# Six normalisations of a two-layer transformer kernel, computed on GpSimd directly behind their power instead of on VectorE a slot later

## The chip, the cores and the metric

One core of a Trainium2 chip. The metric is the device time of one execution in microseconds. In the rows PE is TensorE, PEld its weight load, DVE VectorE, ACT ScalarE, POOL GpSimd and SP SyncE; SPq is the queue from which SP starts transfers.

## The reference

x has 8 sequences of 256 tokens with 256 features. Layer 0 is a masked cross-attention and a ternary linear map on rounded activations, layer 1 a cross-attention with bias, a GELU network and two norms inside, then a mixture of 8 experts. Each of the four starts from a norm without weights:

```python
def _layernorm(x, axis=-1, eps=1e-05):
    m = jnp.mean(x, axis=axis, keepdims=True)
    v = jnp.var(x, axis=axis, keepdims=True)
    return (x - m) / jnp.sqrt(v + eps)
...
    x = x + _L0_xattn_ref(_layernorm(x, axis=-1), ctx_1024, ctx_1024, mask_Bx1xSxS2_ik1, L0_xattn_W, L0_xattn_b)
    x = x + _L0_ffn_ref(_layernorm(x, axis=-1), L0_ffn_weight)
    x = x + _L1_xattn_ref(_layernorm(x, axis=-1), ctx_1024, fside_Bx16xSxS2_0, L1_xattn_Wq, ...)
    x = x + _L1_ffn_ref(_layernorm(x, axis=-1), L1_ffn_Wr, L1_ffn_W1, L1_ffn_b1, L1_ffn_W2, L1_ffn_b2)
```

Inside layer 1's attention block there are two more, `layer_norm(x, g1, be1)` ahead of the GELU network and `layer_norm(x, g2, be2)` behind it. These six are what the change is about.

## The kernel before

**Stages.** The layers come first, for all 8 sequences; then routing (softmax of the logits, a threshold search, the placing of the tokens); then eight experts, one after another, each gathering its tokens by an indirect transfer and adding its result to the output.

**Segments, units, slots.** The attention of one sequence in one layer is a segment: A0 to A7 for layer 0, C0 to C7 for layer 1, in the order A0 A1 A2 C0 A3 C1 A4 C2 A5 C3 A6 C4 A7 C5 C6 C7. A segment has 16 units of two heads and 128 queries. Each engine runs a loop over slots; in slot t PE computes the scores of unit t+2 (ps_s, L383), the transposes of unit t's probabilities (ps_t, L393) and the products with the values of unit t-2 (ps_o, L413); DVE adds mask or bias to the scores of t+2 and finds the row's minimum of the negated scores (neg, neg_max, L659), then the low part of the transposed probabilities of t (p_lo, L666); ACT takes the exponentials of t+1 (probs, L810) and the high part of t (p_hi, L817). Every fourth slot ACT copies eight heads' results (o_raw, L896) and POOL normalises them in three operations (L1023, L1026, L1034) into attn.

**Work beside the units.** Everything else is placed in slots by hand, in `slots_of(b)`: the queries and keys of the next segments, output maps, the quantised map, the GELU network. Each engine's program is written in the order of the slots, an engine takes its instructions strictly in this order, and semaphores order the engines against each other.

**The norms.** Each has a letter: A ahead of layer 0's queries, B ahead of the Hadamard map, C ahead of layer 1's queries, F ahead of the GELU network, G behind it, R ahead of the router. A norm has four steps for a pair of tiles of 128 tokens. DVE: BATCH_NORM_STATS and BATCH_NORM_AGGREGATE (L618, L622), which give mv, mean and variance. POOL: `po_rstd` (L918), an addition of eps and a power of -0.5 (L921, L923) on 128x2 elements. DVE, one slot later (R of b up to 4: three): `ve_ln_apply` (L628), two TENSOR_SCALAR of 128x256 (L633) that subtract the mean and multiply by rstd. Then the user. PE transposes nrm A, B, C, F and R (L327). For G, POOL multiplies by g2 and adds be2 (L1007, L1010) and adds the result to x (L1014), which raises x3_ready.

**Who stands behind x3_ready.** DVE takes R's statistics from this x. SP, whose program is also in slot order, stores x (L1561), and its next transfers follow in its queue: for a later segment, part_h and part_l (the high and low half of keys or queries) go to parts_dram (L1526, L1528) and come back spread over partitions as k_stack and q_stack (L1543, L1555). ACT may write the next part_h (L822) only when the last one has landed in parts_dram.

**Other work of POOL in the layers.** The split of the values into three bf16 parts (`po_split_values`, five steps in five slots), the mask from int32 (L963), part_l of layer 0's keys (L953), the bias of x (L958), x plus the quantised map's result (L978), the kept copy of nrm C (xq_res, L987).

Of the kernel before, what the change touches and what calls it, by code (L numbers as in the profile page):

```python
# [115 lines left out]
def build(nc, a, out):  # L116
    with ExitStack() as ctx:
# [507 lines left out]

        nrm_used = {"A": S["qa_T"], "B": S["hb_T"], "C": S["xc_T"], "F": S["z_T"], "G": S["x3_ready"], "R": S["xr_T"]}

        def ve_ln_apply(ve, k, b, src, dst=None):  # L628
            dst = nrm[k] if dst is None else dst
            ve.wait_ge(ln_rstd[k], b + 1)  # L630
            wait(ve, nrm_used[k], b)
            for t in range(QT):
                ins = nc.vector.tensor_scalar(dst[:, t, :], src(t), mv[k][:, t, 0:1], rstd[k][:, t:t + 1],  # L633
                                              ALU.subtract, ALU.mult)
            ins.then_inc(ln_done[k], 1)

        def xtile(b):
            return lambda t: x_all[:, 2 * b + t, :]

# [36 lines left out]
        def ve_prepare_a(ve, t, b):  # L676
            at = AT[b]
            if t == at["ln_a"]:
                ve.wait_ge(ld[f"x{b}" if b < 2 else "x"], 16)
                ve_ln_stats(ve, "A", b, xtile(b))  # L680
            if t == at["ln_a_apply"]:
                ve_ln_apply(ve, "A", b, xtile(b))
            if t == at["q_a_low"]:
                ve_part_low(ve, part_number(A, b, "q"), ps_m[1][:, :], DK ** -0.5)

        def ve_rest(ve, t, b):
            at = AT[b]
            if t == at["x1"]:
                ve.wait_ge(S["x_biased"], b + 1)
                ve.wait_ge(S["wa_out"], b + 1)  # L690
                nc.vector.tensor_tensor(xpair(b), tokens(ps_m[0]), xpair(b), ALU.add).then_inc(S["x1_ready"], 1)
                ve.wait_ge(S["x1_ready"], b + 1)
                ve_ln_stats(ve, "B", b, xtile(b))
            if t == at["ln_b_apply"]:
                ve_ln_apply(ve, "B", b, xtile(b))
            if t == at["quant"][0]:
                step = b * 4
                ve.wait_ge(S["had_out"], b + 1)
                nc.vector.tensor_reduce(q_amax[:, :], tokens(ps_m[0]), AX_X,
                                        ALU.max, apply_absolute_value=True).then_inc(S["q_step"], 1)  # L700
                ve.wait_ge(S["q_step"], step + 1)
                nc.vector.tensor_scalar(q_scale[:, :], q_amax[:, :], 1e-5, 1.0 / 7.0,
                                        ALU.max, ALU.mult).then_inc(S["q_step"], 1)
                ve.wait_ge(S["q_step"], step + 2)
                nc.vector.reciprocal(q_inv[:, :], q_scale[:, :]).then_inc(S["q_step"], 1)
                ve.wait_ge(S["q_step"], step + 3)
                wait(ve, S["x2_ready"], b)
                for n in range(QT):
                    ins = nc.vector.tensor_scalar(q_rnd[:, n, :], ps_m[0][:, n * D:(n + 1) * D], q_inv[:, n:n + 1],
                                                  ROUND, ALU.mult, ALU.add)  # L710
                ins.then_inc(S["q_step"], 1)
            if t == at["quant"][1]:
                ve.wait_ge(S["q_step"], b * 4 + 4)
                nc.vector.tensor_scalar(q_rnd[:, :, :], q_rnd[:, :, :], -ROUND, 7.0,
                                        ALU.add, ALU.min).then_inc(S["q_capped"], 1)
                ve.wait_ge(S["q_capped"], b + 1)
                wait(ve, S["q_int_T"], b)
                nc.vector.tensor_scalar(q_int[:, :, :], q_rnd[:, :, :], -8.0, None,
                                        ALU.max).then_inc(S["q_int_ready"], 1)
            if t == at["yq"]:  # L720
                ve.wait_ge(S["tern_out"], b + 1)
                for n in range(QT):
                    ins = nc.vector.scalar_tensor_tensor(y_quant[:, n, :], ps_m[0][:, n * D:(n + 1) * D],
                                                         q_scale[:, n:n + 1], w_b_row[:, :], ALU.mult, ALU.mult)
                ins.then_inc(S["yq_ready"], 1)

        def ve_prepare_c(ve, t, b):
            at = AT[b]
            if t == at["ln_c"]:
                ve.wait_ge(S["x2_ready"], b + 1)  # L730
                ve_ln_stats(ve, "C", b, xtile(b))
            if t == at["ln_c_apply"]:
                if b == NB - 1:
                    ve.wait_ge(S["qa_T"], NB)
                else:
                    wait(ve, S["xq_kept"], b)
                ve_ln_apply(ve, "C", b, xtile(b), norm_c(b))
            if t == at["k_low"]:
                ve_part_low(ve, part_number(C, b, "k"), ps_m[0][:, :], 1.0)
            if t == at["q_low"]:  # L740
                ve_part_low(ve, part_number(C, b, "q"), ps_m[1][:, :], DK ** -0.5)

        def ve_finish(ve, t, b):
            at = AT[b]
            if t == at["y"]:
                ve.wait_ge(S["xq_kept"], b + 1)
                ve.wait_ge(S["wo_out"], b + 1)
                nc.vector.tensor_tensor(y_of(b)[:, :, :], tokens(ps_m[0]), xq_res[:, :, :], ALU.add).then_inc(S["y_ready"], 1)
                ve.wait_ge(S["y_ready"], b + 1)
                ve_ln_stats(ve, "F", b, lambda n: y_of(b)[:, n, :])  # L750
            if t == at["ln_f_apply"]:
                ve_ln_apply(ve, "F", b, lambda n: y_of(b)[:, n, :])
            if t == at["y_ffn"]:
                ve.wait_ge(S["yb_ready"], b + 1)
                ve.wait_ge(S["f2_out"], b + 1)
                nc.vector.tensor_tensor(y_of(b)[:, :, :], tokens(ps_m[1]), y_of(b)[:, :, :], ALU.add).then_inc(S["yf_ready"], 1)
            if t == at["ln_g"]:
                ve.wait_ge(S["yf_ready"], b + 1)
                ve_ln_stats(ve, "G", b, lambda n: y_of(b)[:, n, :])
            if t == at["g_scale"]:  # L760
                ve_ln_apply(ve, "G", b, lambda n: y_of(b)[:, n, :])
            if t == at["ln_r"]:
                ve.wait_ge(S["x3_ready"], b + 1)
                ve_ln_stats(ve, "R", b, xtile(b))
            if t == at["ln_r_apply"]:
                wait(ve, S["stored_n"], b * 16)
                ve_ln_apply(ve, "R", b, xtile(b))
            if t == at["logit_copy"]:
                ve.wait_ge(S["logit_out"], b + 1)
                nc.vector.tensor_copy(logits[:, 2 * b:2 * b + 2, :],  # L770
                                      ps_m[1][:, 0:QT * E].rearrange("p (t e) -> p t e", t=QT)
                                      ).then_inc(S["logit_ready"], 1)
# [145 lines left out]
        def po_rstd(po, k, b):  # L918
# [3 lines left out]
            po.wait_ge(ln_eps[k], b + 1)  # L922
            nc.gpsimd.tensor_tensor(rstd[k][:, :], var_eps[k][:, :], half_neg[:, :], ALU.pow).then_inc(ln_rstd[k], 1)  # L923

        def po_split_values(po, k, b, n, step_sem, ready_sem):

            raw = v_raw[k][:, :, :].rearrange("p t (h d) -> p t h d", h=H)
# [17 lines left out]
        def po_prepare_a(po, t, b):  # L945
            at = AT[b]
            if t == at["ln_a"]:
                po_rstd(po, "A", b)
            if t == at["k_a"]:
                n = part_number(A, b, "k")  # L950
                wait(po, S["out_l"], n * 16)
                po.wait_ge(S["part_h"], n + 1)
                nc.gpsimd.tensor_tensor(part_l[:, :, :], ctxT[A][:, :, :], part_h[:, :, :].bitcast(F32),  # L953
                                        ALU.subtract).then_inc(S["part_l"], 1)
# [17 lines left out]
        def po_rest(po, t, b):  # L972
            at = AT[b]
            if t == at["x1"]:
                po_rstd(po, "B", b)
            if t == at["x2"]:
                po.wait_ge(S["yq_ready"], b + 1)
                nc.gpsimd.tensor_tensor(xpair(b), xpair(b), y_quant[:, :, :], ALU.add).then_inc(S["x2_ready"], 1)  # L978

        def po_prepare_c(po, t, b):  # L980
            at = AT[b]
            if t == at["ln_c"]:
                po_rstd(po, "C", b)
            if t == at["xq"]:
                po.wait_ge(ln_done["C"], b + 1)
                wait(po, S["y_ready"], b)
# [8 lines left out]
        def po_finish(po, t, b):  # L995
            at = AT[b]
            if t == at["y"]:
                po_rstd(po, "F", b)
            if t == at["yb"]:
                po.wait_ge(ln_done["F"], b + 1)  # L1000
                nc.gpsimd.tensor_tensor(y_of(b)[:, :, :], y_of(b)[:, :, :], rows[:, 1:2, :].to_broadcast([P, QT, D]),
                                        ALU.add).then_inc(S["yb_ready"], 1)
            if t == at["ln_g"]:
                po_rstd(po, "G", b)
            if t == at["g_scale"]:
                po.wait_ge(ln_done["G"], b + 1)
                nc.gpsimd.tensor_tensor(nrm["G"][:, :, :], nrm["G"][:, :, :], rows[:, 2:3, :].to_broadcast([P, QT, D]),  # L1007
# [6 lines left out]
                nc.gpsimd.tensor_tensor(xpair(b), xpair(b), nrm["G"][:, :, :], ALU.add).then_inc(S["x3_ready"], 1)  # L1014
            if t == at["ln_r"]:
                po_rstd(po, "R", b)

        def po_o_normalise(po, half):

# [752 lines left out]
```

## Time and profile before

| | |
|---|---|
| median of 3 runs | 983.77 us (983.73 to 984.74) |
| profiled execution | 983.23 us, its span 981.4 us |
| PE busy | 769.3 us (78%), 6377 instructions |
| DVE busy | 660.2 us (67%), 2037 |
| ACT busy | 616.5 us (63%), 1275 |
| POOL busy | 430.6 us (44%), 626 |
| mean granted TensorE clock | 0.90 of full speed |

Busy time is the union of an engine's instructions. In rows, "idle before" and the brackets behind a row of a timeline give how long the engine stood still ahead of an instruction and what ended it. The chain that the page follows back from the end reaches 706 us; ahead of that one reads the timeline.

### The profile page before, as it was taken

The numbers are of one execution on the slowest core, as the hardware profiler recorded it, in microseconds if no ns is written. First come the engines' busy times: TensorE is split into PE (matmuls) and PEld (weight loads), VectorE is DVE, ScalarE is ACT, GpSimd is POOL, SyncE is SP. The second block draws the span as 40 slices with busy tenths as digits, with TensorE's granted clock in tenths as the row PEclk, the third lists the DMA queues.
The fourth block names the chain that finished last, engine by engine and source line by source line (L and its number), as shares of the span: only waits on it lengthen the run. The fifth ranks groups of instructions, "written<-read, shape, count | busy, mean of one in ns | idle before, by whom it ended". The sixth has DMA issues, their size and how long they took to land. (4 is left out here: it accounts for less than half of the span.)

```text
span 981.4 us, 19294 instructions
## 1 busy us (share of the span) xinstructions
PE 769.3 (78%) x6377; PEld 676.4 (69%) x6377; DVE 660.2 (67%) x2037; ACT 616.5 (63%) x1275; POOL 430.6 (44%) x626
## 2 busy tenths in 40 slices
PE   0566887887897987987989878878532799999995
PEld 0556776776786776876878768766421588888885
DVE  2686799786885986886787677542176366666651
ACT  1485777787787778679669758762010566666662
POOL 5154245264453554355244244143202456666654
PEclk9798789898998998999899998899655799999998
DMA  8598458668278477566645849200040234455532
GB/s 210 150 263 239 96 109 208 194 134 201 92 158 193 109 161 202 132 142 182 140 118 137 181 136 236 77 22 22 21 129 19 91 107 121 126 130 130 129 65 33
DMA packets 100290, 131.14 MB, mean 134 GB/s; under 512 B 8160, under 2 KB 72160, under 8 KB 100192
## 3 DMA queue, kind: packets, MB, share of 16 engines
q1 hardware_dynamic: 94048, 121.52, 48.8%
q0 software_dynamic: 6144, 8.39, 4.9%
q8 instruction: 52, 0.85, 0.4%
q14 instruction: 46, 0.38, 0.1%
HBM read 104.72 MB, written 25.17 MB: 132 GB/s over the span
## 5 line engine op out<-in xcount | busy, mean ns | idle before, releaser
L810 ACT ACTIVATE probs<-neg,neg_max 128x256 f32<-128x256 f32 x512 | 233.1, 507 | 108.5 <-DVE neg_max L659 105.4
L666 DVE TENSOR_TENSOR p_lo<-ps_t,p_hi 128x512 f16<-128x512 f32 x256 | 176.4, 689 | 108.5 <-ACT p_hi L817 108.4
L393 PE MATMUL ps_t<-ident,probs 128*128 128x128 f32 x1024 | 171.9, 294 | 59.8 <-ACT probs L810 59.3
L383 PE MATMUL ps_s<-k_stack,q_stack 128*128 128x256 f32 x512 | 147.2, 371 | 40.3 <-DMA q_stack<-parts_dram 21.3
L393 PEld LDWEIGHTS ps_t<-ident,probs 128*128 128x128 f32 x1024 | 124.3, 149 | 76.9 <-ACT probs L810 76.6
L817 ACT ACTIVATE p_hi<-ps_t 128x512 f16<-128x512 f32 x256 | 150.5, 588 | 27.5 <-PE ps_t L393 26.2
L383 PEld LDWEIGHTS ps_s<-k_stack,q_stack 128*128 128x128 f32 x512 | 94.6, 205 | 56.6 <-issue 30.8
L659 DVE CUSTOM_DVE_ANT_0 neg<-ps_s,bias_t 128x256 f32<-128x256 f32 x256 | 96.7, 415 | 13.8 <-PE ps_s L383 11.1
L1023 POOL TENSOR_TENSOR o_sum<-o_raw 128x128 f32<-128x128 f32 x64 | 30.2, 472 | 165.4 <-ACT o_raw L896 165.4
L659 DVE CUSTOM_DVE_ANT_0 neg<-ps_s,mask_add 128x256 f32<-128x256 f32 x224 | 84.1, 414 | 22.5 <-PE ps_s L383 22.3
L1329 DVE TENSOR_TENSOR hid_l<-hid_e,hid_h 128x512 fp32r<-128x512 f32 x64 | 69.4, 1115 | 40.2 <-ACT hid_e L1433 21.0
L413 PE MATMUL ps_o<-v_parts,p_hi 128*128 128x49 bf16 x1024 | 90.9, 189 | 0.9 <-DVE p_lo L666 0.9
L413 PE MATMUL ps_o<-v_parts,p_lo 128*128 128x49 bf16 x1024 | 89.4, 187 | 0.0
L1469 POOL DMA_INDIRECT out<-y_g,idx x32 | 52.8, 1649 | 67.7 <-ACT y_g L1447 59.5
L572 PE MATMUL ps_m<-w,hidT 128*128 128x256 f32 x256 | 76.0, 437 | 6.1 <-DVE part_l L673 5.3
L413 PEld LDWEIGHTS ps_o<-v_parts,p_hi 128*128 128x128 f16 x1024 | 79.2, 100 | 1.5 <-issue 1.3
L1399 PE MATMUL ps_o<-w_h,hid_h 128*128 128x256 f32 x256 | 75.3, 294 | 2.8 <-DVE hid_l L1329 2.7
L1399 PE MATMUL ps_o<-w_l,hid_h 128*128 128x256 f32 x256 | 72.3, 283 | 0.0
L1399 PE MATMUL ps_o<-w_h,hid_l 128*128 128x256 f32 x256 | 72.3, 282 | 0.0
L413 PEld LDWEIGHTS ps_o<-v_parts,p_lo 128*128 128x128 f16 x1024 | 68.1, 100 | 4.3
L555 PE MATMUL ps_m<-nrmT,w 128*128 128x256 f32 x256 | 68.8, 397 | 1.1 <-ACT nrmT L869 1.1
L1455 POOL DMA_INDIRECT xg<-normed_dram,idx x32 | 36.3, 1133 | 62.3 <-DVE idx L1302 45.7
(231 smaller groups left out, 1750.9 us busy)
## 6 DMA issues: line engine op xcount, KB each, us to landing
bias_t<-in_bias SPq DMA_DIRECT2D x64, 512.0 KB, 6.7
k_stack<-parts_dram SPq DMA_DIRECT2D x64, 256.0 KB, 4.3
q_stack<-parts_dram SPq DMA_DIRECT2D x128, 128.0 KB, 4.8
parts_dram<-part_h SPq DMA_DIRECT2D x32, 256.0 KB, 3.4
parts_dram<-part_l SPq DMA_DIRECT2D x32, 256.0 KB, 2.6
w1e<-in_w1e SPq DMA_DIRECT2D x8, 1024.0 KB
w2e<-in_w2e SPq DMA_DIRECT2D x8, 1024.0 KB, 5.7
ctxT_A<-in_ctxT SPq DMA_DIRECT2D x8, 256.0 KB, 5.7
```

Of the source, the lines that this page charges most:

```text
L383: ins = nc.tensor.matmul(ps_s[U % 2][:, i * SEQ:(i + 1) * SEQ], q_stack[g % 2][:, h % 2, j, c, qt * P:(qt + 1) * P], k_stack[g % 2][:, j, ...
L393: ins = nc.tensor.matmul(ps_t[U % 2][:, (i * QT + kb) * P:(i * QT + kb + 1) * P], probs[:, U % 2, i, kb * P:(kb + 1) * P], ident[:, :], st ...
L413: ins = nc.tensor.matmul(ps_o[half][:, col:col + VW], part[:, U % 4, (i * QT + kb) * P:(i * QT + kb + 1) * P], v_parts[g % 2][:, kb, h, :] ...
L555: ins = nc.tensor.matmul(ps_m[hc // 2 % 2][:, (hc % 2) * SEQ:(hc % 2 + 1) * SEQ], w_1[:, c, hc * P:(hc + 1) * P], nrmT[:, c, :], start=(c ...
L572: ins = nc.tensor.matmul(ps_m[1][:, tile * D:(tile + 1) * D], hidT[:, hc, tile * P:(tile + 1) * P], w_2[:, hc, :], start=(hc == 0), stop=( ...
L659: ins = nc.vector.tensor_tensor_reduce(neg[:, U % 4, i, :], ps_s[U % 2][:, i * SEQ:(i + 1) * SEQ], add, -1.0, 3.0e38, ALU.add, ALU.min, ne ...
L666: nc.vector.tensor_tensor(p_lo[:, U % 4, :], ps_t[U % 2][:, :], p_hi[:, U % 4, :], ALU.subtract).then_inc(lo_ready, 1)
L810: ins = nc.scalar.activation(probs[:, U % 2, i, :], neg[:, U % 4, i, :], ACT.Exp, bias=neg_max[:, U % 4, i:i + 1], scale=-1.0)
L817: nc.scalar.activation(p_hi[:, U % 4, :], ps_t[U % 2][:, :], ACT.Copy).then_inc(hi_ready, 1)
L1329: nc.vector.tensor_tensor(hid_l[:, hc, :], hid_e[:, hc % 4, :], hid_h[:, hc, :].bitcast(F32), ALU.subtract).then_inc(S["hid_ready"], 1)
L1399: ins = nc.tensor.matmul(ps_o[i][:, (st % 2) * D:(st % 2 + 1) * D], hid[:, hc, st * P:(st + 1) * P], w[:, hc, :], start=(n == 0), stop=(n ...
L1469: nc.gpsimd.indirect_dma_start(out, bass.IndirectOffsetOnAxis(ap=idx[e % 4][:, st:st + 1], axis=0), y_g[:, st, :], None, compute_op=ALU.ad ...
```

## The change

`ve_ln_apply` goes from DVE's program in all its six places, and `po_ln_apply`, the same two TENSOR_SCALAR on POOL, comes into POOL's, directly behind `po_rstd` of the same norm. With it go the waits for the buffer that is written. Semaphores that the users wait for (ln_done) stay, now raised by POOL. In the program this is one slot earlier for A, B, C, F and G; for R it is three slots for b up to 4 and one after that. What stood in `x_biased`, `xq`, `yb` and `g_scale` on POOL with a wait on ln_done keeps it. SP's `store_normed` keeps its slot.

```diff
-        def ve_ln_apply(ve, k, b, src, dst=None):
-            dst = nrm[k] if dst is None else dst
-            ve.wait_ge(ln_rstd[k], b + 1)
-            wait(ve, nrm_used[k], b)
-            for t in range(QT):
-                ins = nc.vector.tensor_scalar(dst[:, t, :], src(t), mv[k][:, t, 0:1], rstd[k][:, t:t + 1],
-                                              ALU.subtract, ALU.mult)
-            ins.then_inc(ln_done[k], 1)
...
-            if t == at["ln_a_apply"]:
-                ve_ln_apply(ve, "A", b, xtile(b))
...
-            if t == at["ln_b_apply"]:
-                ve_ln_apply(ve, "B", b, xtile(b))
...
-            if t == at["ln_c_apply"]:
-                if b == NB - 1:
-                    ve.wait_ge(S["qa_T"], NB)
-                else:
-                    wait(ve, S["xq_kept"], b)
-                ve_ln_apply(ve, "C", b, xtile(b), norm_c(b))
...
-            if t == at["ln_f_apply"]:
-                ve_ln_apply(ve, "F", b, lambda n: y_of(b)[:, n, :])
...
-            if t == at["g_scale"]:
-                ve_ln_apply(ve, "G", b, lambda n: y_of(b)[:, n, :])
...
-            if t == at["ln_r_apply"]:
-                wait(ve, S["stored_n"], b * 16)
-                ve_ln_apply(ve, "R", b, xtile(b))
...
+        def po_ln_apply(po, k, b, src, dst=None):
+            dst = nrm[k] if dst is None else dst
+            po.wait_ge(ln_rstd[k], b + 1)
+            wait(po, nrm_used[k], b)
+            for t in range(QT):
+                ins = nc.gpsimd.tensor_scalar(dst[:, t, :], src(t), mv[k][:, t, 0:1], rstd[k][:, t:t + 1],
+                                              ALU.subtract, ALU.mult)
+            ins.then_inc(ln_done[k], 1)
...
             if t == at["ln_a"]:
                 po_rstd(po, "A", b)
+                po_ln_apply(po, "A", b, xtile(b))
...
             if t == at["x1"]:
                 po_rstd(po, "B", b)
+                po_ln_apply(po, "B", b, xtile(b))
...
             if t == at["ln_c"]:
                 po_rstd(po, "C", b)
+                if b == NB - 1:
+                    po.wait_ge(S["qa_T"], NB)
+                else:
+                    wait(po, S["xq_kept"], b)
+                po_ln_apply(po, "C", b, xtile(b), norm_c(b))
...
             if t == at["y"]:
                 po_rstd(po, "F", b)
+                po_ln_apply(po, "F", b, lambda n: y_of(b)[:, n, :])
...
             if t == at["ln_g"]:
                 po_rstd(po, "G", b)
+                po_ln_apply(po, "G", b, lambda n: y_of(b)[:, n, :])
...
             if t == at["ln_r"]:
                 po_rstd(po, "R", b)
+                wait(po, S["stored_n"], b * 16)
+                po_ln_apply(po, "R", b, xtile(b))
```

## Rows read from the trace of the kernel before

**Rows 1.** Busy time by stage: columns PE, PEld, DVE, ACT, POOL, clock, DMA, GB/s.

```profile
20.00:640.00 620.00, 504.28 (x4564) 447.55 (x4565) 469.73 (x1695) 456.91 (x985) 265.68 (x476) 0.92 0.65 159
```

**Rows 2.** Who waited for whom, 20 to 645 us: total, times, longest.

```profile
DVE p_lo L666 <- ACT p_hi L817: 108.1, 126, 6.1
ACT probs L810 <- DVE neg_max L659: 104.7, 89, 19.1
```

**Rows 3.** Instructions of L633: duration ns min/median/max, first and last start.

```profile
L633 DVE TENSOR_SCALAR nrm_A<-x_all,mv_A,rstd_A x16: 401/419/1352, 8.2 to 443.8; 128x256 f32<-128x256 f32 x16
```

**Rows 4.** POOL's groups by form: busy us, mean ns, idle before and releaser.

```profile
L934 POOL CAST v_parts<-v_raw_A 128x256 bf16<-128x256 f32 x16 | 6.1, 412 | 0.5
L936 POOL TENSOR_TENSOR v_rest<-v_raw_A,v_parts 128x256 f32<-128x256 f32 x16 | 10.4, 674 | 0.7
L987 POOL COPY xq_res<-nrm_A 128x512 f32<-128x512 f32 x1 | 0.6, 611 | 0.0
L963 POOL TENSOR_SCALAR nrm_C<-mask_int 128x512 f32<-128x512 int32 x1 | 1.9, 1943 | 0.1
```

**Rows 5.** Timeline of POOL, units 97 to 101: start us, duration us.

```profile
256.00 0.72 POOL L923 TENSOR_TENSOR rstd_C<-var_eps_C,half_neg 128x2 f32<-128x2 f32 x1
...
257.74 0.40 POOL L1034 TENSOR_TENSOR attn<-o_sum,o_inv 128x128 f32<-128x128 f32 x1
259.33 0.22 POOL L921 TENSOR_SCALAR var_eps_G<-mv_G 128x2 f32<-128x2 f32 x1 [1.18 <-DVE mv_G L622]
259.63 0.71 POOL L923 TENSOR_TENSOR rstd_G<-var_eps_G,half_neg 128x2 f32<-128x2 f32 x1
261.23 1.28 POOL L1007 TENSOR_TENSOR nrm_G<-nrm_G,rows 128x512 f32<-128x512 f32 x1 [0.89 <-DVE nrm_G L633]
...
263.94 1.27 POOL L1014 TENSOR_TENSOR x_all<-x_all,nrm_G 128x512 f32<-128x512 f32 x1
```

**Rows 6.** Timeline of SP's queue in the same stretch.

```profile
265.24 0.38 SPq L1561 DMA_DIRECT2D out<-x_all  x1
265.73 0.40 SPq L1526 DMA_DIRECT2D parts_dram<-part_h  x1
```

**Rows 7.** Timeline of ACT in the same stretch.

```profile
268.19 0.60 ACT L822 ACTIVATE part_h<-ps_m 128x512 fp32r<-128x512 f32 x1 [2.13 <-DMA parts_dram<-part_h]
```

**Rows 8.** Timelines of DVE and PE behind a B.

```profile
308.64 0.78 DVE L633 TENSOR_SCALAR nrm_B<-x_all,mv_B,rstd_B 128x256 f32<-128x256 f32 x2
...
310.16 2.04 PE L572 MATMUL ps_m<-w,hidT 128*128 128x256 f32 x4 [1.34 <-DVE part_l L673]
```

**Rows 9.** Timelines of DVE and ACT around an R, an F behind it.

```profile
275.60 0.95 DVE L633 TENSOR_SCALAR nrm_R<-x_all,mv_R,rstd_R 128x256 f32<-128x256 f32 x2
...
277.98 0.92 ACT L810 ACTIVATE probs<-neg,neg_max 128x256 f32<-128x256 f32 x2 [0.55 <-DVE neg_max L659]
```

**Rows 10.** Timeline of DVE at the last units.

```profile
652.35 0.73 DVE L633 TENSOR_SCALAR nrm_R<-x_all,mv_R,rstd_R 128x256 f32<-128x256 f32 x2 [0.86 <-issue]
```

**Rows 11.** Timelines of DVE and POOL at segment 7's G and R.

```profile
700.59 0.73 DVE L633 TENSOR_SCALAR nrm_G<-y_attn,mv_G,rstd_G 128x256 f32<-128x256 f32 x2 [1.14 <-POOL rstd_G L923]
...
701.41 1.26 POOL L1007 TENSOR_TENSOR nrm_G<-nrm_G,rows 128x512 f32<-128x512 f32 x1 [0.85 <-DVE nrm_G L633]
...
706.81 0.71 POOL L923 TENSOR_TENSOR rstd_R<-var_eps_R,half_neg 128x2 f32<-128x2 f32 x1
...
708.40 1.12 PE L327 MATMUL ps_m<-ident,nrm_R 128*128 128x128 f32 x4 [10.82 <-DVE nrm_R L633]
```

**Rows 12.** Timelines of POOL, DVE, SP's queue and PE at the start.

```profile
8.15 1.25 POOL L953 TENSOR_TENSOR part_l<-ctxT_A,part_h 128x512 fp32r<-128x512 f32 x1
...
8.20 1.68 DVE L633 TENSOR_SCALAR nrm_A<-x_all,mv_A,rstd_A 128x256 f32<-128x256 f32 x2 [1.26 <-POOL rstd_A L923]
...
9.43 0.33 SPq L1528 DMA_DIRECT2D parts_dram<-part_l  x1
...
29.46 1.19 PE L383 MATMUL ps_s<-k_stack,q_stack 128*128 128x256 f32 x4 [18.35 <-DMA q_stack<-parts_dram]
```

## What I predicted

> **What bounds the kernel now.** I read the busy time by stage first [rows 1]. The layers take the stretch to 708 us; behind them, to 981 us, come routing and the experts, which the change doesn't touch. From 20 to 640 us PE is busy 504 of 620 us, DVE 470, ACT 457, POOL 266: no engine is full, and POOL has the most room. So the pace is set by waits in a ring, and the next view is who waits for whom [rows 2]. DVE waits 108 us for ACT's p_hi, ACT waits 105 us for DVE's neg_max. An operation taken from DVE thus pays where ACT waits for DVE directly behind it, and nothing where PE has no gap or a transfer ends last. That can only be read stage by stage, so I went through the timeline of all 256 units with the 48 normalisations marked. From unit 80 on it repeats every 32 units (about 78 us).
>
> **What one normalisation is.** Two TENSOR_SCALAR of 128x256 on DVE; a pair takes 0.73 to 0.95 us in the timeline [rows 8, 9, 11], more when POOL reads SBUF at the same time: one reached 1352 ns [rows 3]. 48 pairs are about 37 us of DVE. The change also drops the hand-over POOL to DVE, and for G back to POOL. No wait is new on POOL for stats (POOL waited for them for its power already); the added waits are on buffers (nrm_used, xq_kept, stored_n) whose readers by program order lie 8 or more slots back, so I cost them at nothing. What they would hold is everything later on POOL: attn, x2, x3.
>
> **The unknown: a pair on POOL, P.** No row has a float TENSOR_SCALAR of 256 columns on POOL. Nearest rows [rows 4]: CAST of 256 columns 412 ns; TENSOR_TENSOR of 256, 674 ns; TENSOR_SCALAR of 512 columns with two operations, from int32 and with a comparison, 1943 ns; COPY of 512, 611 ns. Floor: two CASTs, started as closely as the trace's cast pairs (a pair spans 0.76 us). Ceiling: the per-column rate of the int32 row, 1.94 us for 512 columns in all. The int32 row is the same operation with two ALU steps but also converts and compares, the cast has no arithmetic; two plain steps on one float input should lie between, about at 0.64 us each. I take P = 1.2 us, near the two-input pair (1.3).
>
> The Trainium skill ("GPSIMD Engine Reference", section 4.1 Engine selection) says that one-input operations on GpSimd run at roughly line rate and only two-input ones about 2x slower than VectorE. The cast and copy rows agree, the int32 row does not. By the rule P would be 0.76 and the result that of the first rival.
>
> **Where POOL's chain is the path: C, G and x3, five times.** In units 97 to 101 (and 129, 161, 193, 225) C's normalisation of one segment and G's of another fall together. DVE has no gap there and both applies are in its row, so it looks like the place to gain. But the stretch ends on something else: SP, in order, holds the store of x behind x3_ready and the transfer parts_dram<-part_h behind the store. x3 (L1014) ends at 265.21, the store issues at 265.24, part_h at 265.73 [rows 5, 6], and ACT stands idle 2.13 us until that transfer has landed [rows 7]; PE and DVE wait behind ACT. So only the end of x3 counts.
> After the change, in the times of before: rstd_C ends 256.72; C's pair follows (256.78 + P); then POOL's three attn operations, which took 256.68 to 258.14, now end at 258.2+P (they no longer wait for o_inv). G's stats come 0.7 us earlier (nrm_C no longer stands ahead of them on DVE) and no longer hold. var_eps_G to the end of rstd_G is 1.01 us (259.33 to 260.34), then G's pair, then multiply, add and x3: 3.98 us from 261.23 to 265.21. Sum: 258.2+P + 0.05 + 1.01 + 0.06 + P + 0.06 + 3.98 = 263.3+2P, against 265.2. The end of x3 moves by 2P - 1.9: +0.5 us at P = 1.2, -0.35 at 0.76, +2.0 at 1.94. Five times: **+2.5 us** (-1.8 to +10). The 1.5 us of DVE freed here are hidden behind this transfer.
>
> **Where DVE's row is the path.** B, behind ACT's stall around the GELU: nrm_B (0.78 in its row, 0.70 until part_l starts) stands ahead of part_l, for which PE's f2 waits with a gap of 1.34 us [rows 8], and ahead of neg, for which ACT waits 1.6. The gain passes whole: 0.7 us, five times (230, 308, 387, 466, 550 us). The three earlier ones (87, 127, 158) have ACT gaps of 1.5 to 2.0 but PE nearly full: 0.5 each. Together **-5.1**. B on POOL then runs inside the stall (rstd_B ends 4 us before DVE gets to it).
> R and F, adjacent on DVE for 1.5 us (the R is shown) [rows 9]: ACT waits only 0.55 us for the neg behind them and PE has gaps of some 0.3 us in the next 10: 0.3 each, six times: **-1.8**.
> C of segments 0, 1, 6 and the A's: PE has no gap; 0.1 to 0.3 each, **-1.5** in all.
> End of the units, R of segment 5: DVE waits for x3, later 0.86 us for rstd_R, with the last p_lo queued behind nrm_R [rows 10]. Without the apply p_lo goes 1.4 us earlier, at P = 1.2 with x3 unmoved; PE then follows to 1.0: **-1.0**.
>
> **The tail, bare.** From 673 us there is no attention; G and R of segments 6 and 7 are one serial chain. G: 0.03 + 0.73 + 0.09 us before, between the end of rstd_G (700.56) and POOL's next start (701.41); now 0.13 + P. R: rstd_R ends 707.52, PE starts 708.40 [rows 11]; now 0.12 + P. Four of them: 4P - 3.0 = **+1.8 us** (0 to +4.8). F of both segments is covered by PE's f2.
>
> **Start.** Segment 0's A now stands on POOL ahead of part_l<-ctxT_A, with SP's part_l transfer behind that (9.43) and all k_stack, q_stack loads behind it in order; PE's first scores wait for the q_stack load [rows 12]. nrm_A itself gains (its pair took 1.68, next to POOL's operation). part_l comes P+0.06 later; SP's next load, the first of k_stack, waits for part_h's landing anyway, the third one and all behind it for part_l's, so I count two thirds, **+0.8 us** (0 to 1.3).
>
> **Sum** at P = 1.2: -5.1 -1.8 -1.5 -1.0 = -9.4; +2.5 +1.8 +0.8 = +5.1; together -4.3 us. As a function: about 14P - 21. The profiled execution took 983.23 us (span 981.4), the median of the runs is 983.77: 983.77 - 4.3 = **979.4 us**.
>
> **Rivals.**
> (1) POOL at the cast's rate, P = 0.76: 14 x 0.76 - 21 = -10.4, with the smaller terms taken singly about -11: 972.8 us. For it: the cast and copy rows. Against: the int32 row of the very operation.
> (2) Slower: POOL becomes the bound through x3. P = 1.94: five times +2.0, the tail +4.8, the start +1.3, against gains of 9.1: +7, 990.7 us. It decides from P = 1.51, where the sum is zero (+0.2% from 1.65). For it: the int32 row, 3.3 ns per column above the 0.22 us of an operation on two columns [rows 5]. Against: its conversion and comparison.
> (3) DVE's freed time doesn't arrive, since PE, at 81%, closes the gaps: half of 9.4 lost, -4.3 + 4.7 = +0.4: 984.2 us, no change that can be measured. For it: PE has no gap over 0.3 us in most stretches with an apply. Against: PE's own wait for part_l.
>
> **How the numbers follow.** This kernel's runs can tell some 0.2% (2 us) from no change. Forecast 0.32; rival 1, 0.20; rival 2, 0.28; rival 3, 0.20. Faster is the forecast and rival 1, 0.52; same 0.20; slower 0.28. The range leaves out the far ends of P: 972.5 to 989.
>
> **What would show it.** The pair on POOL: its duration decides, read first. x3's end to be at 263.3+2P in the stretch around 255 us, relative to st_C; ACT's wait for parts_dram<-part_h grows or shrinks by 2P - 1.9 plus what DVE gained before it (so to 3 us or more at P = 1.2). The gap of 1.34 us at f2 shrinks to 0.6. The tail from 673 to 708 us is 1.8 us longer. L714 and L718 on DVE may lengthen beside POOL's reads; that costs little. I am wrong if attn or va_ready comes late for PE, or if x3's transfer isn't what holds ACT.

## The result and the profile after

The kernel after takes 1005.34 us (median; 1003.44 to 1013.83), the kernel before 983.75: ratio 1.0239, 95% interval 1.0206 to 1.0272. I had forecast 979.4 us and a range up to 989. The profiled execution of after took 1006.00 us, its span is 1004.2 (before 983.23 and 981.4).

The price of the moved operation comes first. The busy time of each engine in the page of after, then the two TENSOR_SCALAR of a norm on POOL among its groups by form (busy us, mean ns, idle before):

```profile
PE 770.2 (77%) x6377; PEld 682.1 (68%) x6377; DVE 627.2 (62%) x1941; ACT 615.7 (61%) x1275; POOL 546.5 (54%) x722
```

```profile
L904 POOL TENSOR_SCALAR nrm_A<-x_all,mv_A,rstd_A 128x256 f32<-128x256 f32 x16 | 19.5, 1230 | 0.8
L904 POOL TENSOR_SCALAR nrm_B<-x_all,mv_B,rstd_B 128x256 f32<-128x256 f32 x16 | 19.5, 1227 | 0.8
```

One takes 1.23 us, so a pair is P = 2.44 us, twice my value (1.2) and above my ceiling (1.94). POOL is 116 us busier for 33 us less on DVE. Yet POOL is only 54% busy, so what counts is again where it stands in the ring. POOL in units 97 to 101 of after (start us, duration us), to be laid beside [rows 5]:

```profile
256.60 0.72 POOL L897 TENSOR_TENSOR rstd_C<-var_eps_C,half_neg 128x2 f32<-128x2 f32 x1
257.48 2.44 POOL L904 TENSOR_SCALAR nrm_C<-x_all,mv_C,rstd_C 128x256 f32<-128x256 f32 x2 [0.17 <-issue]
...
260.96 0.40 POOL L1028 TENSOR_TENSOR attn<-o_sum,o_inv 128x128 f32<-128x128 f32 x1
261.33 0.23 POOL L895 TENSOR_SCALAR var_eps_G<-mv_G 128x2 f32<-128x2 f32 x1
261.64 0.72 POOL L897 TENSOR_TENSOR rstd_G<-var_eps_G,half_neg 128x2 f32<-128x2 f32 x1
262.47 2.44 POOL L904 TENSOR_SCALAR nrm_G<-y_attn,mv_G,rstd_G 128x256 f32<-128x256 f32 x2
...
267.69 1.26 POOL L1006 TENSOR_TENSOR x_all<-x_all,nrm_G 128x512 f32<-128x512 f32 x1
```

From the end of rstd_C to the end of x3 it was 8.49 us (256.72 to 265.21), now it is 11.63 (257.32 to 268.95): 3.14 us longer, where my 2P - 1.9 gives 2.98. Then SP's queue, ACT and DVE in the same stretch, beside [rows 6] and [rows 7]:

```profile
268.98 0.38 SPq L1555 DMA_DIRECT2D out<-x_all  x1
269.48 0.40 SPq L1520 DMA_DIRECT2D parts_dram<-part_h  x1
```

```profile
271.94 0.60 ACT L796 ACTIVATE part_h<-ps_m 128x512 fp32r<-128x512 f32 x1 [6.31 <-DMA parts_dram<-part_h]
```

```profile
268.99 0.75 DVE L618 BATCH_NORM_STATS2 st_R<-x_all 128x6 f32<-128x256 f32 x2 [3.32 <-POOL x_all L1006]
```

ACT's wait grew from 2.13 to 6.31 us, and DVE now waits 3.32 us for x3 as well; in segments 0 to 4 it had no such wait before. Summed from 80 to 645 us (total, times, longest), first ACT's wait in before, then both in after:

```profile
ACT part_h L822 <- DMA parts_dram<-part_h: 17.4, 6, 5.7
```

```profile
ACT part_h L796 <- DMA parts_dram<-part_h: 37.0, 6, 8.7
...
DVE st_R L618 <- POOL x_all L1006: 16.1, 5, 3.3
```

By the starts of p_lo and of the later steps the 22.8 us between the two traces lie so: up to unit 96 0.6, from unit 96 to unit 255 14.6, from there to the last logits 8.5, experts -0.9. To see where in a cycle of 32 units they lie, I took from each trace the start of p_lo at its slots and averaged three cycles (those that begin with units 96, 128, 160). The kernels are explained below; us:

| kernel | slots 0-5 (x3) | slots 6-11 | whole cycle |
|---|---|---|---|
| before | 16.30 | 13.35 | 78.6 |
| after | 19.36 | 13.25 | 80.8 |
| C and G on POOL | 19.49 | 13.77 | 82.0 |
| G alone | 17.96 | 13.79 | 80.8 |
| C alone | 17.88 | 13.46 | 79.8 |
| before, store later | 14.07 | 13.35 | 76.3 |
| after, store later | 16.06 | 12.98 | 77.0 |
| the same, R's statistics later | 12.96 | 16.02 | 77.4 |
| B on POOL, store later | 14.09 | 13.33 | 75.4 |

All that after loses in these cycles it loses in the six slots of x3: +3.1 us there, -0.8 in the others. The next two cycles (from units 192 and 224) are longer by 4.0 and 3.9 us.

Another way for POOL to cost time would be to slow DVE's instructions beside it. It does not show here: without the moved operations, the durations of DVE's instructions add up to 0.6 us more than before, and p_lo takes 689 ns in both kernels.

### The profile page after: what moved, and what is told of

Read it like the earlier page. It is cut to its first block and busy times, and to the rows that moved or that the text cites. A ratio compares the mean times of both kernels' runs of the same rounds, so it can differ in the third digit from the quotient of the medians.

```text
span 1004.2 us, 19294 instructions
## 1 busy us (share of the span) xinstructions
PE 770.2 (77%) x6377; PEld 682.1 (68%) x6377; DVE 627.2 (62%) x1941; ACT 615.7 (61%) x1275; POOL 546.5 (54%) x722
## 5 line engine op out<-in xcount | busy, mean ns | idle before, releaser
L393 PEld LDWEIGHTS ps_t<-ident,probs 128*128 128x128 f32 x1024 | 126.4, 151 | 85.9 <-ACT probs L784 85.2
L1393 PE MATMUL ps_o<-w_h,hid_h 128*128 128x256 f32 x256 | 75.4, 295 | 2.8 <-DVE hid_l L1323 2.7
```

What stands on the lines that cost most here:

```text
L393: ins = nc.tensor.matmul(ps_t[U % 2][:, (i * QT + kb) * P:(i * QT + kb + 1) * P], probs[:, U % 2, i, kb * P:(kb + 1) * P], ident[:, :], st ...
L1393: ins = nc.tensor.matmul(ps_o[i][:, (st % 2) * D:(st % 2 + 1) * D], hid[:, hc, st * P:(st + 1) * P], w[:, hc, :], start=(n == 0), stop=(n ...
```

## The experiments

All are made from the kernel before, and each norm can be put on either engine. An interval behind a ratio is the 95% interval of that ratio; single executions of one kernel differ by up to 12 us, so a difference of a few us between two whole traces is no finding. Slots 0 to 5 repeat far better: 19.36 us in each of the first four cycles of after. "Before" is timed again in each job (983.7 to 985.0 us).

### The same places, cheaper operations

The copy leaves out the subtraction and the multiplication, the second form leaves out the multiplication.

```diff
-                ins = nc.gpsimd.tensor_scalar(dst[:, t, :], src(t), mv[k][:, t, 0:1], rstd[k][:, t:t + 1],
-                                              ALU.subtract, ALU.mult)
+                ins = nc.gpsimd.tensor_copy(dst[:, t, :], src(t))                                           # first run
+                ins = nc.gpsimd.tensor_tensor(dst[:, t, :], src(t), mv[k][:, t, 0:1].to_broadcast([P, D]), ALU.subtract)  # second
```

> All six on GpSimd as in the change, but each operation is a TENSOR_COPY of 128x256, so the subtraction and the multiplication are left out; a pair should take 0.76 us instead of 2.44. Theory 1 (only the price P of the pair was mis-sized, the rest of the sum holds, 14P - 21): 10 us faster than before, 971 to 976 us. Theory 2 (the changed kernel is 8 us above what the sum gives at P = 2.44, so the gains on DVE's row were overstated or POOL's order costs something apart from P): only 1 to 3 us faster.

977.71 us, ratio 0.9925 (0.9895 to 0.9956).

> All six on GpSimd, each operation a TENSOR_TENSOR that subtracts the mean (broadcast over 256 columns), so the multiplication by rstd is left out; a pair should take 1.3 us. This is the P that was forecast. Theory 1: 2 to 4 us faster than before. Theory 2: 5 us slower.

983.63 us, ratio 0.9998 (0.9971 to 1.0026).

A pair of copies took 0.74 us, a pair of the two-input form 1.19. Both results lie between their two theories. So there are three points for the change as a function of P, beside my formula: P = 0.74, measured -6.7 us (-10.3 to -4.3), formula -10.6; P = 1.19, -0.8 (-2.9 to +2.6) against -4.3; P = 2.44, +21.6 against +13.2. The zero lies near P = 1.25 (I said 1.51), and the line is steeper at its upper end: 18 us per us of P against 13. The second run has the very P that I took, 1.2 us, and it brings nothing that can be measured, not the 4.3 us forecast. The size of P is thus the larger miss, not the only one.

### Which norms cost

```diff
+        def on_pool(k, b):
+            return k in "CG"        # second run: k in "ABFR"; third: k == "G"; fourth: k == "C"
```

> Only C and G on GpSimd, the others on DVE as before; nothing left out. Theory 1 (the loss is x3 ending 3 us later five times, plus the bare tail's two G at 1.7 each): 16 to 20 us slower than before, and ACT's wait for parts_dram<-part_h about 5 us or more in the stretch around 265 us. Theory 2 (POOL's load as a whole delays attn, values and the last units): below 11 us slower.

1007.9 us, ratio 1.0229 (1.0194 to 1.0264): 23.5 us slower (19.1 to 26.0), as the first theory has it and somewhat more.

> Only A, B, F and R on GpSimd, C and G on DVE as before; nothing left out. Theory 1 (B and the R, F pairs gain 7 us on DVE's row; the tail's two R cost 1.6 each, the start 1.6): 2 to 5 us faster than before. Theory 2: slower than before by 3 us or more.

984.71 us, ratio 1.0009 (0.9975 to 1.0043): between the two theories.

The whole loss comes from C and G (+23.5 us). A, B, F and R together are worth nothing that can be measured here; in the kernel after, beside C and G, they are worth 1007.9 - 1005.3 = 2.6 us by the medians, and by the ratios (1.0229 against 1.0239, with intervals that overlap) nothing. I had counted some 9 us of gains. At the measured P the two R in the tail take 3.5 of them back and the start 1.7, which leaves -3.8 us, outside the interval (-2.5 to +4.2). The trace of this run is of an execution of 979.69 us, near the fastest of its kernel (979.22 to 989.67): up to the last unit it is 6.3 us shorter than the trace of before, and 3.8 longer from there to the last logits. So in this one execution the gains arrive and the tail takes its part back; in the median they don't.

> The kernel before, with G's normalisation alone on POOL. T1 (x3's end moves by P less the 0.83 us of the hand-over and pair on DVE, so 1.6 us at P = 2.44, and all of it is paid, five times; the bare tail pays 1.77 us twice, as the trace of after shows it): 8.0 + 3.5, 11.5 us slower than before. T2 (a first delay of x3 costs more than its length, since a stretch at half the TensorE clock gets longer with it): 15 to 18 us slower. T3 (a delay of 1.6 us is covered, only both norms together are not): under 6 us slower.

1000.84 us, ratio 1.0169 (1.0125 to 1.0213): 16.6 us slower.

> The kernel before, with C's normalisation alone on POOL. T1 (C's pair holds attn and through it var_eps_G: 258.2 + P + 0.05 = 260.7 against 259.33, so x3 ends 1.36 us later, five times, less 1 us for DVE in the other segments): 5 to 7 us slower than before; with G alone this makes some 18 where C and G together took 23.5. T2 (more than its length): 9 to 12 us slower, and the two single costs add up to 23.5 or more. T3 (DVE's 0.7 us freed ahead of st_G take up the delay): under 3 us slower.

993.11 us, ratio 1.0100 (1.0047 to 1.0153): 8.8 us slower.

G alone fits its second theory. C alone lies between its first (5 to 7) and its second (9 to 12), and its interval (4.6 to 15.1 us) holds both; for G the interval is 12.3 to 21.0. The two single costs add up to 25.4, as the second theory of C has it, against 23.5 for both together, a difference within the noise. In slots 0 to 5 each pays what its own term says: G +1.66 us (1.61 expected), C +1.58 (1.36). What each costs beyond that lies elsewhere. For G alone, take the last layers' stage, from the last unit to G's statistics of segment 6, where no norm has been moved but G's, behind it. Columns as in [rows 1]; first before, then G alone, then the kernel before with only the store of x moved (described below), where this stage isn't touched either:

```profile
653.00:674.00 21.00, 16.07 (x80) 13.23 (x80) 3.99 (x12) 6.64 (x11) 3.51 (x6) 0.92 0.04 12
```

```profile
664.60:689.30 24.70, 19.49 (x81) 15.51 (x80) 4.25 (x12) 6.84 (x11) 3.50 (x6) 0.72 0.03 11
```

```profile
640.50:662.80 22.30, 17.25 (x81) 14.02 (x80) 4.18 (x12) 6.70 (x11) 3.51 (x6) 0.85 0.04 12
```

80 or 81 matmul records, nearly the same time on DVE, ACT and POOL, and 21.0, 24.7 and 22.3 us at mean granted clocks of 0.92, 0.72 and 0.85: the stage is the longer the lower its clock. In C alone one finds the like in units 236 to 239, first before, then C alone:

```profile
604.56:613.20 8.64, 7.88 (x78) 7.11 (x77) 5.71 (x23) 7.51 (x18) 3.33 (x7) 1.00 1.09 307
```

```profile
609.34:622.95 13.61, 10.78 (x78) 9.57 (x77) 5.88 (x23) 7.53 (x18) 3.29 (x7) 0.75 0.93 237
```

The same 78 matmul records keep PE busy 2.9 us longer at the lower clock, and PE stands still 2.83 us instead of 0.76 ahead of the last segment's first scores. But the run with nine extra operations in slot 0 (next section), at 983.15 us as fast as before, has 12.13 us and a clock of 0.86 in these four units. So a jump of this size in one trace is no proof that C's place caused it.

By the records of the clock, the time at its lower level (1.2 GHz) between 40 and 660 us was 97 us before, 126 in after, 119 in G alone, 113 with C and G, 106 with C alone, and 102 in that run of 983.15 us. That the clock explains what C and G cost beyond their terms isn't shown: I could not change the clock alone.

### What the operation costs on POOL

Nine operations on POOL in slot 0, when it has nothing else to do; m and r are columns of constants.

```diff
+            ts(hidT[:, 0, :], src, m, r, ALU.subtract, ALU.mult)
+            ts(hidT[:, 1, :], src, m, None, ALU.subtract)
+            ts(hidT[:, 2, :], src, 0.5, 2.0, ALU.subtract, ALU.mult)
+            ts(hidT[:, 3, :], src, 0.5, None, ALU.add)
...
+            nc.gpsimd.tensor_copy(xq_res[:, 0, :], src)
+            nc.gpsimd.tensor_tensor(xq_res[:, 1, :], src, r.to_broadcast([P, D]), ALU.mult)
+            ts(y_attn[:, :, :], x_all[:, 0:2, :], m, r, ALU.subtract, ALU.mult)
```

> The kernel before with nine extra operations on POOL behind the zeroing of q_stack in slot 0, where POOL has nothing else to do (22 to 34 us), each into a buffer not yet in use: TENSOR_SCALAR of 256 columns with two operations by pointers, one operation by pointer, two by immediates, one by immediate; two by pointers and one by immediate on 128 columns; COPY and a TENSOR_TENSOR with a broadcast column of 256; two operations by pointers on 512. Before measured COPY 128x512 611 ns and TENSOR_TENSOR 128x256 674 ns, after 1228 ns for the two-step form of 256 columns. T1 (the second ALU step is what costs, as I assumed from TENSOR_TENSOR's rate): one step about 0.65 us, two steps 1.2 whether by pointer or immediate. T2 (the pointers cost): by pointer 1.2 or so with one step too, by immediates 0.4 to 0.6. T3 (the operation as such, 3.9 ns per column): all four about 1.2, and 512 columns 2.2. The time of the kernel: unchanged within 2 us.

The timeline of POOL in this run (the first number behind the start is the duration in us):

```profile
22.06 1.23 POOL L1145 TENSOR_SCALAR hidT<-x_all,half_neg 128x256 f32<-128x256 f32 x1
23.29 0.92 POOL L1146 TENSOR_SCALAR hidT<-x_all,half_neg 128x256 f32<-128x256 f32 x1
24.27 1.07 POOL L1147 TENSOR_SCALAR hidT<-x_all 128x256 f32<-128x256 f32 x1
25.32 0.87 POOL L1148 TENSOR_SCALAR hidT<-x_all 128x256 f32<-128x256 f32 x1
26.18 0.80 POOL L1149 TENSOR_SCALAR q_rnd<-x_all,half_neg 128x128 f32<-128x128 f32 x1
...
27.43 0.39 POOL L1151 COPY xq_res<-x_all 128x256 f32<-128x256 f32 x1
27.80 0.61 POOL L1152 TENSOR_TENSOR xq_res<-x_all,half_neg 128x256 f32<-128x256 f32 x1
28.40 2.08 POOL L1153 TENSOR_SCALAR y_attn<-x_all,half_neg 128x512 f32<-128x512 f32 x1
```

None of the three theories alone holds: the form as such makes the most (one step by immediate 0.87 against 0.39 for a copy), the second step adds 0.20 to 0.31, pointers 0.05 to 0.16. From 256 to 512 columns the two-step form grows by 0.85 us, 3.3 ns per column, over a fixed part of 0.38. That is the slope that I had read off the int32 row of [rows 4] and then explained away by its conversion and comparison: that row less the 0.22 us of two columns gives 3.36 ns per column, 0.22 + 256 x 3.36 ns gives 1.08 us, and the two-step form by immediates took 1.07. The fault was also in the ceiling: 1.94 us was the price of one instruction on 512 columns, while a pair is two on 256, with the fixed part twice and the pointers on top: 2 x 1.23 = 2.46. The Trainium skill ("GPSIMD Engine Reference", section 4.1 Engine selection) has one-input operations at roughly line rate. The copy agrees (0.39 us for 256 columns), TENSOR_SCALAR doesn't: on POOL its two-step form takes 1.23 us, where DVE takes 0.42 [rows 3] and where POOL's own two-input operation of the same size takes 0.61.

### By which way x3 holds the others

SP stores x five slots later for segments 0 to 4, so that part_h doesn't queue behind x3_ready. First in the kernel before, then with all six norms on POOL.

```diff
-                if t == at["x3"] + 1:
+                if t == at["x3"] + 1 + (5 if b < 5 else 0):
                     store_x(b)
```

> The kernel before, where only SP's store of x goes five slots later for segments 0 to 4, so that the next part_h no longer queues behind x3_ready. T1 (the chain x3, store, part_h to parts_dram, ACT sets the end of this stretch in the kernel before too): ACT's wait of 2.1 us for parts_dram falls under 0.5 in each cycle of 32 units, the first six slots of the cycle from 16.3 us to about 14.5, in all 7 to 12 us faster. T2 (the stall is given back at the next segment's first scores or to the TensorE clock): under 3 us faster.

970.5 us, ratio 0.9859 (0.9824 to 0.9893). The same part_h on ACT as in [rows 7] no longer waits:

```profile
266.14 0.61 ACT L830 ACTIVATE part_h<-ps_m 128x512 fp32r<-128x512 f32 x1
```

So the chain that I had named was the bound of this stretch already in the kernel before: 13.2 us of 983.7 hang on the place of the store of x in SP's queue, in five segments.

> The same later store, with all six normalisations on POOL as in the kernel after. T1 (what C and G cost comes through the store in SP's queue): the first six slots of the cycle fall from 19.4 us to about 15 to 16, in all 12 to 20 us faster than the kernel after, so 986 to 993, the rest of the loss being the tail (4 x 2.44 - 3.0 = 6.8 us) and DVE's wait for x3 ahead of R's statistics. T2 (x3 hurts through DVE's statistics of R, which stand ahead of p_lo, or through POOL's attn): it stays over 1000.

977.32 us, ratio 0.9924 (0.9894 to 0.9953): 28 us under after, more than expected, with slots 0 to 5 at 16.06 us as expected. Against the kernel before with the same store it is still 6.8 us slower; it was 21.6 without. By the two traces this rest lies behind the units: the last unit starts 1.4 us earlier than in the kernel before with the later store, and from there to the last logits it takes 9.1 us longer, the tail. In slots 0 to 5 it is still 2.0 us slower per cycle (16.06 against 14.07). That is the second way, in the timelines of DVE and ACT:

```profile
267.89 0.75 DVE L618 BATCH_NORM_STATS2 st_R<-x_all 128x6 f32<-128x256 f32 x2 [3.33 <-POOL x_all L1045]
```

```profile
269.68 0.91 ACT L818 ACTIVATE probs<-neg,neg_max 128x256 f32<-128x256 f32 x2 [3.38 <-DVE neg_max L664]
```

R's statistics stand in DVE's order ahead of neg and p_lo, and ACT waits behind them. The next run moves them one slot for segments 0 to 4:

```diff
+    if b < 5:
+        at.update(ln_r=c + 54)
```

> All six norms on POOL and the later store, and in addition R's statistics on DVE (and its power and norm on POOL) one slot later for segments 0 to 4, so that DVE's p_lo and neg don't stand behind x3. T1 (the second way by which x3 holds the others is DVE's wait of 3.3 us ahead of st_R, behind which ACT waits 3.4 us for neg_max): that wait falls under 0.5, the first six slots of the cycle from 16.1 us to about 14, the kernel 7 to 11 us under the one with the later store alone (977.3), so 966 to 970. T2 (POOL itself is late there, with attn or the norms): under 3 us gained.

984.42 us, ratio 0.9996 (0.9974 to 1.0017): 7 us slower than without the move. A miss, and the table says why nothing was gained: slots 0 to 5 fell by 3.1 us, as the first theory has it, and slots 6 to 11 rose by 3.0. It doesn't say why the kernel got slower; the trace is of the slowest of its executions (989.98 of 981.47 to 989.98), and that part stays open. POOL, then PE, there:

```profile
271.06 2.44 POOL L949 TENSOR_SCALAR nrm_R<-x_all,mv_R,rstd_R 128x256 f32<-128x256 f32 x2
273.46 0.23 POOL L931 TENSOR_SCALAR var_eps_F<-mv_F 128x2 f32<-128x2 f32 x1
273.78 0.72 POOL L933 TENSOR_TENSOR rstd_F<-var_eps_F,half_neg 128x2 f32<-128x2 f32 x1
274.60 2.43 POOL L949 TENSOR_SCALAR nrm_F<-y_attn,mv_F,rstd_F 128x256 f32<-128x256 f32 x2
```

```profile
277.09 1.11 PE L329 MATMUL ps_m<-ident,nrm_F 128*128 128x128 f32 x4 [0.79 <-POOL nrm_F L949]
```

POOL has no idle time from G's pair to the end of F's, some 15 us. With DVE no longer held at x3, F's norm comes sooner on DVE, not on POOL, where R's pair stands ahead of it. An engine that is half idle over the kernel is the bound of this stretch.

### The tail alone

The kernel after, with the norms of segments 6 and 7 left on DVE (`b < 6` on POOL).

> The kernel after, but the norms of segments 6 and 7 stay on DVE as before. T1 (the serial tail pays for each pair at its full price): segments 6 and 7 took 8.5 us more from the last unit to the last logits (14.2 by the formula 4P - 3 gives 6.8 of it), so the kernel comes out 6 to 9 us under after, 996 to 999. T2 (the tail's loss is only what the layers pass on): under 3 us gained.

999.27 us, ratio 1.0155 (1.0125 to 1.0185): 6.1 us under after by the medians, 8.3 by the ratios. In its trace the way from the last unit to the last logits is 0.9 us longer than before, 8.5 in after.

### What of the change is worth keeping

With the later store: B, F and A, R of segments 1 to 4 on POOL; then B alone; then all six for segments 0 to 5 but A of segment 0, with R's statistics later.

```diff
+            return k in "BF" or (k in "AR" and 1 <= b <= 4)    # first run
+            return k == "B"                                     # second
+            return b < 6 and (k, b) != ("A", 0)                 # third
```

> The later store, with B and F of all segments and A and R of segments 1 to 4 on POOL, the others on DVE as before. T1 (what POOL takes over where x3 is not near is worth what I costed, 0.7 us per B and 0.3 per R and F): 3 to 6 us faster than the later store alone. T2 (these gains are lost to the clock and the segment boundary, as with A, B, F and R on POOL without the later store, which came out at 1.0009 of before): within 2 us of the later store alone.

964.98 us, ratio 0.9802 (0.9753 to 0.9851).

> The later store, with B alone on POOL. T1 (B's gain passes whole, as I costed it: 0.7 us in five segments, 0.5 in three): 5 us under the later store alone (970.5), so 965.5, with PE's gap ahead of f2 at 308 us down from 1.2 to 0.6 us. T2 (the gap closes, but the next slots or the segment's boundary take it back): gap closed, and no more than 2 us gained.

965.79 us, ratio 0.9816 (0.9787 to 0.9844).

> Later store and later R statistics, with all six norms on POOL for segments 0 to 5 except A of segment 0, DVE for segments 6 and 7 and that A. T1: the gains of the two schedule edits and of the bare tail add up: 957 to 962. T2 (with x3 no longer in the way nothing is left of the choice of engine): within 2 us of the kernel with the later store and B, F, A, R on POOL (965.0).

977.84 us, ratio 0.9929 (0.9905 to 0.9952); a miss for both theories, by the same stretch of POOL as in the run with R's statistics later (slots 6 to 11: 16.01 us).

B alone takes the later store from 970.5 to 965.8 us: 4.7 us, where my term was 5.1. PE's gap ahead of f2 at 308 us in that run, beside [rows 8] (1.34 before; 1.23 with the later store alone):

```profile
307.51 2.05 PE L572 MATMUL ps_m<-w,hidT 128*128 128x256 f32 x4 [0.51 <-DVE part_l L678]
```

A, F and R add nothing to it that can be measured (965.0 and 965.8; the interval of the first is 9.6 us wide, so a gain of 2 or 3 us isn't ruled out). The kernel with the later store and B on POOL is faster than both kernels of this case, by 18 us than before and by 40 than after.

## Why the prediction was wrong

**What bounds the kernel.** Right: no engine, but a ring. A place that bounds it was named right too: moving the store took 13.2 us off the kernel before.

**P, the step that failed.** Taken at 1.2 us with a ceiling of 1.94; measured 2.44. I had the row of the very operation and set it aside for the rows of other operations, and counted its fixed part once for two instructions. By 14P - 21 the right P gives +13.2 us, 997.0. The sign and over half of the size hang on this step: of the 25.9 us between forecast (-4.3) and result (+21.6), some 17.5 are P by my own formula, 3.5 are missing already at P = 1.19, and 4.9 more are missing between there and 2.44. The formula itself was rounded: the terms add up to 14.7P - 21.9, which is +13.9 us at P = 2.44, and B's three gains of 0.5 and five of 0.7 make 5.0, not 5.1.

**x3, 2P - 1.9.** The mechanism was right, the size too: 3.14 us measured in the trace against 2.98, 3.1 us per cycle. The rival of a slower kernel through x3 was the right case; its price was too low, since P was bounded too low. The second way by which x3 acts, st_R ahead of neg on DVE, I had not named: it is covered as long as ACT's wait is the longer one, and takes over once the store is moved.

**The gains in DVE's row, -9.4.** The gap at f2 shrank as I said, from 1.34 us to 0.52 in after. But A, B, F and R together brought 0 to 3 us beside C and G, and nothing on their own (interval -2.5 to +4.2 us, where the terms leave -3.8). With the store out of the way B brought 4.7 us, against a term of 5.1, and the rest nothing that can be measured. So B's term was right in size with the store moved. The terms of R, F, C and A (-3.3) and of the end of the units are too small to be told from nothing by these runs, and none is confirmed. This is my third rival, a freed time that doesn't arrive, and it held beside the second. What takes B's gain back in the kernel before isn't settled. The lower clock lasted 102 us in the trace with A, B, F and R on POOL against 97 before, but that trace is of a fast execution, so it says little.

**The tail, 4P - 3.0.** By the measured P it is 6.8 us; measured 8.5 in the trace, and 6.1 (by the ratios 8.3) by taking it back. Segment 7 shows it bare. POOL waits no more for DVE between rstd_G and the multiplication, but the pair is in its own row:

```profile
719.88 0.72 POOL L897 TENSOR_TENSOR rstd_G<-var_eps_G,half_neg 128x2 f32<-128x2 f32 x1
720.71 2.43 POOL L904 TENSOR_SCALAR nrm_G<-y_attn,mv_G,rstd_G 128x256 f32<-128x256 f32 x2
723.22 1.26 POOL L999 TENSOR_TENSOR nrm_G<-nrm_G,rows 128x512 f32<-128x512 f32 x1
...
732.01 1.11 PE L327 MATMUL ps_m<-ident,nrm_R 128*128 128x128 f32 x4 [14.40 <-POOL nrm_R L904]
```

From the end of rstd_G to the multiplication 2.62 us against 0.85 [rows 11], from the end of rstd_R to PE 2.65 against 0.88: 1.77 each, P - 0.67 where I had P - 0.72 and P - 0.76.

**The start, +0.8.** Covered: PE's first scores stand at 29.61 us against 29.46 [rows 12], though part_l on POOL comes 2.3 us later.

```profile
29.61 1.19 PE L383 MATMUL ps_s<-k_stack,q_stack 128*128 128x256 f32 x4 [17.88 <-DMA q_stack<-parts_dram]
```

**The waits on buffers, counted at nothing.** Right: ahead of all 48 pairs together POOL stands still 2.3 us, all of it issue (0.17 us at a time), and no wait.

**What stays open.** C and G cost 8.8 and 16.6 us alone, where their terms give 6 and 11.5, though each pays in x3's slots what its term says. For C the term lies within the interval of the measurement (4.6 to 15.1), for G just below it (12.3 to 21.0), and both together lie above theirs. One stage of G's excess, 3.7 us, goes with a lower clock. The rest is not attributed.

## What to carry to other kernels

Price a moved operation by the row of the same operation, even where that row has another type or a comparison, and per instruction: a pair has the fixed part twice. Before moving work to the engine with the most room, look for the stretch in which that engine already carries the chain; there its mean load says nothing, and here the delay was paid in full (3.14 us of x3, 3.1 per cycle). If a wait ends on a transfer, read what stands ahead of it in its queue: moving the store of x brought more (13 us) than any choice of engine, and it decided what the choice of engine was worth.

## What the runs showed of the hardware

- TENSOR_SCALAR of 256 float columns on POOL takes 1.23 us with two steps by pointers and 0.87 with one by immediate, where a copy takes 0.39 and a two-input operation 0.61. On DVE the two-step form took 0.42 [rows 3].
- The two-step form costs POOL 3.3 ns per column over 0.38 us. With int32 input and a comparison it is 3.4 ns, if the 0.22 us of an operation on two columns is its fixed part.
- The stage behind the last unit, with 80 or 81 matmul records, took 21.0 us at a mean granted clock of 0.92, 22.3 at 0.85 and 24.7 at 0.72, though no edit touched it; 78 matmul records of units 236 to 239 kept PE busy 7.88 us at 1.00, 9.45 at 0.86 and 10.78 at 0.75.
